# Maxima matmuls of an attention kernel with 32 rows instead of 64, and a Q image without zero rows

## The chip, the cores and the metric

The kernel runs on one NeuronCore of one Trainium2 chip. The metric is device time in microseconds (us), the median of repeated runs. Before the change it is 1701.23 us, the median of three runs (1700.1 to 1705.75).

## The reference, cut to what matters

The model is one "macaron" layer over 8 sequences of 512 tokens with 128 features: half a feed-forward block, an attention block, and the same feed-forward block again. The feed-forward block is itself an attention with 16 heads of 8 features over the whole sequence, followed by a mixture of 8 experts of which each token uses one.

```
def block(x):                       # _L0_ffn_ref
    x = x + _msa(_layernorm(x, ln1_w, ln1_b), w_qkv, w_proj)
    x = x + _moe_mlp(_layernorm(x, ln2_w, ln2_b), gate_w, gate_b, w1, w2)
    return x
x = x + 0.5 * block(_layernorm(x))
x = x + _L0_attn_ref(_layernorm(x), w_q, w_k, w_v, w_o)    # 16 heads, 4 of keys, RoPE
x = x + 0.5 * block(_layernorm(x))
```

Each attention is softmax(q k^T / sqrt(8)) v, for 16 heads with 8 features, on 512 queries and 512 keys, in float32. There are 3 x 8 = 24 such attentions in all, each of 16 heads.

## The kernel before, in words

The program is a setup, a `stream` of 8 sequences (first block), `experts`, a `stream` of 16 (the attention block and the second block's attention), `experts` again, and `finish`. The change touches only `stream` and the buffers it uses.

Inside `stream`, the 16 heads of a sequence are handled in G = 4 groups of J = 4 heads. One group of one sequence is a "head group" n; the first stream has 32 of them and the second 64. For each head group the kernel makes two passes over the scores:

- The maxima pass (`max_score`, L687): for each of 4 blocks of 128 queries (`qt`) and each of the 4 heads j, one matmul of Q against all 512 keys. VectorE then takes the row maxima of two such 128x512 results in one instruction (`take_max`, L1032).
- The score pass (`score`, L703): the transposed product, 128 keys against 512 queries, with the negative maxima already inside it. ScalarE exponentiates each result (L1008), and the matmuls of `weigh` (L715) multiply the probabilities with V.

Q and K of a head occupy rows of the 128-row memory. Heads with j even lie in rows 0 to 63, those with j odd in rows 64 to 127 (`TILE = 64`). Of each 64 rows, the first 32 (`ROWS = 4 * HD`) hold the 8 features of the head four times over, as high and low parts in every combination, which gives float32 precision from the faster `float32r` matmul. Rows 32 and 33 of Q hold the high and low part of the maxima, and all rows of K from 32 on hold -1, so the score matmul subtracts the maximum for free. The score pass must multiply these rows. The maxima pass, which runs before the maxima exist, must not see an old maximum there: `parts(j)` gives it all 64 rows, and the Q image that is loaded for each head group has 48 rows (`IMAGE`), of which the last 16 are zeros. To supply them, a DMA issued by ScalarE at the start (L979) writes zeros into the DRAM scratch `q_scratch`, SyncE waits for it (`zeroed`, L537), and SyncE writes zeros for the first head group by hand (L540), once per stream.

The order on each engine is written out. On TensorE, `step(n, kt)` is the steady state and has two half-steps. Each half-step issues two score matmuls of head group n and two maxima matmuls of head group n + 2, in the order maxima, score, maxima, score (or score, maxima, score, maxima), on alternating 64-row halves, and then the eight recorded passes of half a `weigh`. So there are 8 half-steps in a head group, 96 head groups, and 768 half-steps; in the last two head groups of each stream there is no later group, so 736 half-steps mix both kinds. `group(n, kt)` adds other work between the steps (transposes, projections, gate). Two maxima results go to VectorE per half-step, two score results to ScalarE. The maxima of head groups 0 and 1 are made ahead of the first step, without scores between them.

SyncE loads each head group's Q and K (`load`) four groups ahead, and writes the maxima into rows 32 and 33 of Q (`rows_of_max`, L524).

Of the kernel before, what the change touches and what calls it, by code (L numbers as in the profile page):

```python
# [19 lines left out]
F32 = mybir.dt.float32  # L20
# [6 lines left out]
P = 128  # L27
# [5 lines left out]
NG = B * G  # L33
# [9 lines left out]
KSLOT = PAIRS * S  # L43
TILE = 64
ROWS = 4 * HD
IMAGE = 48
VCOLS = G * QT * J * V1
VSLOTS = 3
RING = 4
# [3 lines left out]
SLOTS = 5  # L53
# [292 lines left out]
def stream(nc, c, a, label, kinds):  # L346
# [6 lines left out]
    with ExitStack() as ctx:  # L353
# [18 lines left out]
        def parts(j):  # L372

            r = TILE * (j % 2)
            return slice(r, r + TILE)

        def mcol(n, j, qt):

            return 16 * (n % 2) + 8 * (j % 2) + 4 * (j // 2) + qt
# [116 lines left out]
        @block.sync  # L496
        def _(sp):
            def load(n):
                if n >= SLOTS:
                    sp.wait_ge(s.scores, QT * J * (n - SLOTS + 1))  # L500
                g = n % SLOTS
                if n == 1 or n % G == 0:
                    stored(sp, 0, n // G + 1)
                for tile in range(2):
                    sp.dma_start(c.Q[TILE * tile:TILE * tile + IMAGE, g * KSLOT:(g + 1) * KSLOT].bitcast(F32),
                                 c.q_scratch[n % NG, tile, :, :]).then_inc(s.q_loaded[g], 16)
                if n == 1 or n % G == 0:
                    stored(sp, 1, n // G + 1)
                for tile in range(2):
                    for copy in range(2):  # L510
                        r = TILE * tile + 2 * HD * copy
                        sp.dma_start(c.K[r:r + 2 * HD, g * KSLOT:(g + 1) * KSLOT].bitcast(F32),
                                     c.k_scratch[n % NG, tile, :, :]).then_inc(s.k_loaded[g], 16)

            def rows_of_max(n):

                g = n % SLOTS
                if n:
                    released(sp, "rows", n)
                else:  # L520
                    sp.wait_ge(s.first, 2)
                for tile in range(2):
                    r = TILE * tile + ROWS
                    sp.dma_start(c.Q[r:r + 2, g * KSLOT:(g + 1) * KSLOT].bitcast(F32).rearrange("i (a n) -> i a n", n=P),  # L524
                                 c.maxT[16 * tile:16 * tile + 16, n % 2 * P:(n % 2 + 1) * P].bitcast(F32))\
                        .then_inc(s.max_rows[g], 16)

            if gathers:
                for b in range(EARLY + 1):
                    load_outputs(sp, c, b, s.gathered[b])  # L530
            later = later_loads(c, a) if label == 0 else []
            if label == 0:
                for b in range(1, B):
                    load_x(sp, c, a, b)
                sp.wait_ge(c.q_clear, 1)
                sp.wait_ge(c.k_clear, 1)
                sp.wait_ge(c.zeroed, 16)  # L537
            for tile in range(2):
                r = TILE * tile + ROWS
                sp.dma_start(c.Q[r:r + IMAGE - ROWS, 0:KSLOT].bitcast(F32).rearrange("r (o d) -> r o d", o=8),  # L540
                            c.zero[0:IMAGE - ROWS, :].rearrange("r (o d) -> r o d", o=1).broadcast_to((IMAGE - ROWS, 8, KSLOT // 8))).then_inc(s.q_loaded[0], 16)
            whole_ready(sp, 0, 0)
            straight(sp, 0, 0)
            for i in range(2):
                sp.wait_ge(s.lo[i], 1)
                straight(sp, i, 1)
            for i in range(2):
                store(sp, i, 0, s.first_stored[i], (1,))
            for n in range(1, 4):
                load(n)  # L550
            rows_of_max(0)
            for n in range(last):
                if n + 1 < last:
                    rows_of_max(n + 1)
                if n + 4 < last:
                    load(n + 4)
                if n == 0 and label == 0:
                    late_loads(sp, c, a)
                if n >= 1 and later:
                    dst, src = later.pop(0)  # L560
                    sp.dma_start(dst, src).then_inc(c.rest, 16)
            for g in range(SLOTS):
                sp.wait_ge(s.max_rows[g], 32 * len(range(g, last, SLOTS)))
            if label == 0:
                sp.wait_ge(c.rest, 16 * len(later_loads(c, a)))
            write_tails(sp, 0)
            sp.wait_ge(s.tails, 16 * E)
# [104 lines left out]
        def _(pe):  # L672
# [8 lines left out]
            def fill(ins, *name):  # L681
                t = turns[name]
                ins.then_inc(s.filled, t.end - t.first)

            def max_score(n, qt, j):
                bank = bank_for("max", n, qt, j)
                fill(nc.tensor.matmul(bank, q4[parts(j), n % SLOTS, j // 2, qt * P:(qt + 1) * P],  # L687
                                      k4[parts(j), n % SLOTS, j // 2, :], start=True, stop=True), "max", n, qt, j)

            def turn_max(n):  # L690

# [128 lines left out]
                        project(kind, i)  # L820

            def loaded(n):
                pe.wait_ge(s.q_loaded[n % SLOTS], 32 * (n // SLOTS + 1) + 128 * (n % SLOTS == 0))
                pe.wait_ge(s.k_loaded[n % SLOTS], 64 * (n // SLOTS + 1) + 64 * (n % SLOTS == 0))

            def maxima(n, qt):
# [47 lines left out]
        def _(act):  # L874
# [99 lines left out]
                act.wait_ge(c.weights, 16 * c.first_loads)  # L974
            if label:
                nc.scalar.activation(c.warm[:, :], c.zero[:, 0:1], ACT.Sqrt)
            else:
                act.wait_ge(c.x_loaded[0], 16)
                act.dma_start(c.q_scratch[:, :, ROWS:IMAGE, :].rearrange("g t r n -> (g t) (r n)"),  # L979
                              c.zero[:, :].rearrange("p (o d) -> p o d", o=1).broadcast_to((P, 16 * NG * (IMAGE - ROWS) // P, KSLOT // 8)))\  # L980
                    .then_inc(c.zeroed, 16)
            def roots(b):
                for i in range(1 + plan.ffn(b)):
                    act.wait_ge(s.var_ready, sum(1 + plan.ffn(x) for x in range(b)) + i + 1)
# [408 lines left out]
def build(nc, a, out):  # L1393
    with ExitStack() as ctx:
# [6 lines left out]
        c.x_loaded = [ctx.enter_context(nc.semaphore(f"x_loaded{b}")) for b in range(B)]  # L1401
        c.late_loads = 3
        c.q_clear, c.k_clear, c.v_clear = (ctx.enter_context(nc.semaphore(n)) for n in ("q_clear", "k_clear", "v_clear"))
        c.rest, c.zeroed = ctx.enter_context(nc.semaphore("rest")), ctx.enter_context(nc.semaphore("zeroed"))
        c.X, c.Y, c.N = sb("X", [P, B * S]), sb("Y", [P, B * S]), sb("N", [P, NT * W])
        c.rows = c.N[:, :].rearrange("p (t w) -> p t w", w=W)
        c.Q, c.K = (sb(n, [P, SLOTS * KSLOT], F32R) for n in ("Q", "K"))
# [9 lines left out]
        c.rstd, c.root, c.minus_half = sb("rstd", [P, 2 * QT]), sb("root", [P, 2 * QT]), sb("minus_half", [P, QT])  # L1417
        c.normed, c.zT, c.swap, c.turned, c.added = (sb(n, [P, S]) for n in ("normed", "zT", "swap", "turned", "added"))
        c.full, c.hi, c.lo = (sb(n, [P, 2 * S]) for n in ("full", "hi", "lo"))
        c.zero = sb("zero", [P, KSLOT // 8])  # L1420
        c.ident, c.upper, c.ones = sb("ident", [P, P]), sb("upper", [P, P]), sb("ones", [P, P])
        c.maxima = sb("maxima", [P, 32])
        c.split = sb("split", [P, 64], F32R)
# [10 lines left out]
        c.blocks, c.thresh, c.down = sb("blocks", [P, NBLK]), sb("thresh", [P, NT]), sb("down", [P, E])  # L1434
        c.banks = banks = ctx.enter_context(nc.psum_tensor("banks", [P, 8 * 512], F32))
        c.bank = [banks[:, i * 512:(i + 1) * 512] for i in range(8)]
        c.q_scratch = nc.dram_tensor("q_scratch", [NG, 2, IMAGE, KSLOT], F32).ap()
        c.k_scratch = nc.dram_tensor("k_scratch", [NG, 2, 2 * HD, KSLOT], F32).ap()
        c.sorted_x = nc.dram_tensor("sorted_x", [E * REGION + E * P, W], F32).ap()
        c.by_token = nc.dram_tensor("by_token", [NT * P + 2 * E * P, D], F32).ap()  # L1440
# [59 lines left out]
```

## Time and profile before

| | us |
|---|---|
| median of three runs | 1701.23 |
| the profiled execution, own time | 1694.1 |
| its span | 1692.4 |
| TensorE matmul busy | 1440.0 (85%) |
| TensorE weight loads busy | 657.9 (39%) |
| VectorE busy | 1212.0 (72%) |
| ScalarE busy | 1097.7 (65%) |
| GpSimd busy | 625.1 (37%) |

Durations come from one profiled execution, whose own time is 1.7 us more than its span and 7.1 us below the median.
### The profile page before, as it was taken

What the parts mean: (1) busy time and instruction counts of PE and PEld (TensorE: products, weight loads), DVE (VectorE), ACT (ScalarE), POOL (GpSimd) and SP (SyncE); (2) the same over time, 40 slices, a digit from 0 to 9 for tenths busy, and PEclk for the clock granted to TensorE, in tenths of its full rate; (3) what the DMA queues carried; (4) which work ended last, traced back from release to release, by engine and by line L of the source; (5) the groups of instructions that cost most, each with busy time, mean ns of one, the idle gap of its engine ahead of it and who ended that gap; (6) DMA issues with size and microseconds to landing.
All of it is one profiled execution on the core that took longest, in us unless ns stands there. A gap on an engine that the chain in (4) does not pass through costs nothing. (4 is left out here: it accounts for less than half of the span.)

```text
span 1692.4 us, 34258 instructions
## 1 busy us (share of the span) xinstructions
PE 1440.0 (85%) x11860; PEld 657.9 (39%) x11860; DVE 1212.0 (72%) x1961; ACT 1097.7 (65%) x2048; POOL 625.1 (37%) x964
## 2 busy tenths in 40 slices
PE   1899999998964992699999999999999999992994
PEld 1333333333333771233333333333343343332673
DVE  4788888888812444588888888888888888853334
ACT  1377877777742431288888888887877777770441
POOL 2323254432242341454444452233334452125332
PEclk8599999999976995699999999999999999995997
DMA  6545443442001212433324334334234333201114
GB/s 189 121 109 123 105 99 84 108 112 66 24 8 48 57 49 71 107 94 79 94 76 104 91 86 102 87 75 99 64 86 96 92 76 79 55 9 33 53 55 120
DMA packets 99543, 139.07 MB, mean 82 GB/s; under 512 B 26160, under 2 KB 69936, under 8 KB 99376
## 3 DMA queue, kind: packets, MB, share of 16 engines
q1 hardware_dynamic: 60768, 82.65, 19.4%
q0 software_dynamic: 24016, 45.57, 10.8%
q10 hardware_dynamic: 14592, 8.67, 1.7%
q8 instruction: 100, 1.64, 0.4%
q14 instruction: 67, 0.55, 0.1%
HBM read 78.64 MB, written 55.23 MB: 79 GB/s over the span
## 5 line engine op out<-in xcount | busy, mean ns | idle before, releaser
L1032 DVE TENSOR_REDUCE maxima<-banks 128x2 f32<-128x1024 f32 x768 | 923.9, 1222 | 190.4 <-PE banks L687 184.9
L1008 ACT ACTIVATE work<-banks 128x512 f32<-128x512 f32 x1536 | 828.7, 597 | 132.7 <-PE banks L703 119.3
L687 PE MATMUL banks<-K,Q 64*128 64x512 f32 x1536 | 574.6, 463 | 70.9 <-DVE maxima L1032 33.8
L703 PE MATMUL banks<-Q,K 64*128 64x512 f32 x1536 | 571.3, 453 | 11.3 <-ACT work L1008 10.6
L715 PE MATMUL banks<-work,V 128*9 128x256 f32 x6144 | 478.0, 383 | 1.9 <-ACT work L1008 0.8
L687 PEld LDWEIGHTS banks<-K,Q 64*128 64x128 f32 x1536 | 230.7, 190 | 229.5 <-DVE maxima L1032 109.9
L703 PEld LDWEIGHTS banks<-Q,K 64*128 64x128 f32 x1536 | 230.1, 186 | 196.3 <-issue 134.3
L715 PEld LDWEIGHTS banks<-work,V 128*9 128x9 f32 x6144 | 91.4, 88 | 276.5 <-issue 210.7
L1350 DVE COPY work<-banks 128x512 f32<-128x512 f32 x80 | 55.3, 692 | 130.0 <-PE banks L1298 125.7
L612 POOL TENSOR_TENSOR lo<-full,hi 128x512 fp32r<-128x512 f32 x44 | 56.3, 1280 | 246.5 <-issue 97.6
L1272 POOL DMA_INDIRECT by_token<-work x80 | 76.6, 957 | 151.2 <-DVE work L1355 150.5
L105 POOL TENSOR_SCALAR root<-moments 128x4 f32<-128x4 f32 x36 | 8.4, 232 | 272.2 <-DVE moments L1108 190.4
L1328 ACT ACTIVATE work<-banks,ln 128x128 f32<-128x128 f32 x80 | 36.6, 457 | 96.8 <-PE banks L1286 96.8
L1292 PE MATMUL banks<-w,work 128*128 x160 | 92.4, 660 | 1.2 <-ACT work L1328 0.5
L1306 PE MATMUL banks<-w,work 128*128 x640 | 84.8, 275 | 0.3 <-issue 0.3
L1334 ACT ACTIVATE work<-banks 128x512 f32<-128x512 f32 x80 | 47.8, 597 | 47.6 <-PE banks L1292 38.9
L1306 PEld LDWEIGHTS banks<-w,work 128*128 128x128 f32 x640 | 77.7, 192 | 0.7 <-issue 0.7
L599 POOL DMA_INDIRECT sorted_x<-N,pos x64 | 64.3, 1004 | 28.1 <-issue 14.6
L619 POOL TENSOR_TENSOR Y<-Y,added 128x512 f32<-128x512 f32 x16 | 20.6, 1286 | 129.3 <-ACT added L933 129.3
L724 PE MATMUL banks<-ident,outT 128*128 128x128 f32 x384 | 62.8, 286 | 6.2 <-DVE maxima L1032 4.6
L901 ACT ACTIVATE full<-banks 128x512 f32<-128x512 f32 x48 | 28.7, 597 | 58.8 <-PE banks L742 58.0
L883 ACT ACTIVATE outT<-banks 128x512 f32<-128x512 f32 x96 | 58.2, 606 | 2.3 <-PE banks L715 2.3
(172 smaller groups left out, 1354.5 us busy)
## 6 DMA issues: line engine op xcount, KB each, us to landing
Q<-q_scratch SPq DMA_DIRECT2D x188, 192.0 KB, 3.5
K<-k_scratch SPq DMA_DIRECT2D x376, 64.0 KB
q_scratch<-hi POOLq DMA_DIRECT2D x44, 256.0 KB, 4.7
q_scratch<-lo POOLq DMA_DIRECT2D x44, 256.0 KB, 6.8
k_scratch<-hi POOLq DMA_DIRECT2D x22, 256.0 KB, 4.6
k_scratch<-lo POOLq DMA_DIRECT2D x22, 256.0 KB, 6.4
work<-sorted_x SPq DMA_DIRECT2D x80, 66.0 KB
q_scratch<-zero ACTq DMA_DIRECT2D x1, 4096.0 KB, 19.7
```

The lines of the kernel that those rows point to most:

```text
L599: nc.gpsimd.indirect_dma_start(c.sorted_x[:, :], bass.IndirectOffsetOnAxis(ap=c.pos[:, t:t + 1], axis=0), c.rows[:, t, :], None).then_inc( ...
L612: nc.gpsimd.tensor_tensor(lo[i].bitcast(F32R), full[i], hi[i], ALU.subtract).then_inc(s.lo[i], 1)
L687: fill(nc.tensor.matmul(bank, q4[parts(j), n % SLOTS, j // 2, qt * P:(qt + 1) * P], k4[parts(j), n % SLOTS, j // 2, :], start=True, stop=T ...
L703: nc.tensor.matmul(scp[x % EXPS][:, :], k4[parts(j), n % SLOTS, j // 2, kt * P:(kt + 1) * P], q4[parts(j), n % SLOTS, j // 2, :], start=Tr ...
L715: ins = nc.tensor.matmul(outp[32 * j:32 * j + V1, q], v4[:, n // G % VSLOTS, kt, n % G, j, :], prob[:, kt, j, q], start=(kt == 0 and half ...
L724: ins = nc.tensor.transpose(bank[:, t * P:(t + 1) * P], c.outT[:, t * P:(t + 1) * P], c.ident[:, :])
L883: nc.scalar.activation(c.outT[:, :], outp[:, :], ACT.Copy).then_inc(s.out_copied, 1)
L1008: nc.scalar.activation(prob[:, kt, j ^ 1, :], scp[x % EXPS][:, :], ACT.Exp, scale=SCALE).then_inc(s.probs, 1)
L1032: nc.vector.tensor_reduce(c.maxima[:, at:at + 9:8], c.banks[:, k * S:(k + 2) * S].rearrange("p (m n) -> p m n", m=2), AX.X, ALU.max).then_ ...
L1272: nc.gpsimd.indirect_dma_start(c.by_token[:, :], bass.IndirectOffsetOnAxis(ap=x_sb[i % ring][:, D:D + 1].bitcast(U32), axis=0), y_sb[i % r ...
L1292: nc.tensor.matmul(hp[i % 2][:, :], uT[i % 2], cols(c.w1, at, HID), start=True, stop=True).then_inc(s.hidden, 1)
L1306: ins = nc.tensor.matmul(yp[i % 2][:, 0:D], hT[i % 2][:, t * P:(t + 1) * P], cols(c.w2, at + t * D, D), start=(t == 0), stop=(t == HT - 1))
```

## The change

The maxima matmuls use a new slice `heads(j)`, the first 32 rows of each half, where old maxima can't reach them. The Q image in DRAM and each load of it shrink from 48 to 32 rows (192 KB to 128 KB). The ScalarE DMA that writes zeros, the SyncE wait for it, and the four SyncE DMAs of zeros are gone; the count that TensorE waits for in slot 0 is adapted. The score matmuls still use 64 rows.

```
+        def heads(j):
+            r = TILE * (j % 2)
+            return slice(r, r + ROWS)
...
-                    sp.dma_start(c.Q[TILE * tile:TILE * tile + IMAGE, g * KSLOT:(g + 1) * KSLOT].bitcast(F32),
+                    sp.dma_start(c.Q[TILE * tile:TILE * tile + ROWS, g * KSLOT:(g + 1) * KSLOT].bitcast(F32),
                                  c.q_scratch[n % NG, tile, :, :]).then_inc(s.q_loaded[g], 16)
...
                 sp.wait_ge(c.k_clear, 1)
-                sp.wait_ge(c.zeroed, 16)
-            for tile in range(2):
-                r = TILE * tile + ROWS
-                sp.dma_start(c.Q[r:r + IMAGE - ROWS, 0:KSLOT]...,
-                            c.zero[0:IMAGE - ROWS, :]...).then_inc(s.q_loaded[0], 16)
             whole_ready(sp, 0, 0)
             straight(sp, 0, 0)
...
-                fill(nc.tensor.matmul(bank, q4[parts(j), n % SLOTS, j // 2, qt * P:(qt + 1) * P],
-                                      k4[parts(j), n % SLOTS, j // 2, :], start=True, stop=True), "max", n, qt, j)
+                fill(nc.tensor.matmul(bank, q4[heads(j), n % SLOTS, j // 2, qt * P:(qt + 1) * P],
+                                      k4[heads(j), n % SLOTS, j // 2, :], start=True, stop=True), "max", n, qt, j)
...
-                pe.wait_ge(s.q_loaded[n % SLOTS], 32 * (n // SLOTS + 1) + 128 * (n % SLOTS == 0))
+                pe.wait_ge(s.q_loaded[n % SLOTS], 32 * (n // SLOTS + (n % SLOTS > 0)) + 128 * (n % SLOTS == 0))
...
-            else:
-                act.wait_ge(c.x_loaded[0], 16)
-                act.dma_start(c.q_scratch[:, :, ROWS:IMAGE, :]..., c.zero[:, :]...).then_inc(c.zeroed, 16)
...
-        c.q_scratch = nc.dram_tensor("q_scratch", [NG, 2, IMAGE, KSLOT], F32).ap()
+        c.q_scratch = nc.dram_tensor("q_scratch", [NG, 2, ROWS, KSLOT], F32).ap()
```

The order of TensorE's instructions stays as it was. This is the changed kernel's TensorE program at an early step of the first stream; `L686` is `max_score` (L687 before), `L702` is `score` (L703 before), `L714` is `weigh` (L715 before), and 128x512 is the size of the result:

```order
L686 MATMUL banks<-K,Q 128x512
L702 MATMUL banks<-Q,K 128x512
L686 MATMUL banks<-K,Q 128x512
L702 MATMUL banks<-Q,K 128x512
L714 MATMUL banks<-work,V 9x256 x4
L702 MATMUL banks<-Q,K 128x512
L686 MATMUL banks<-K,Q 128x512
L702 MATMUL banks<-Q,K 128x512
L686 MATMUL banks<-K,Q 128x512
L714 MATMUL banks<-work,V 9x256 x4
```

Nothing moved here: 32-row and 64-row matmuls now alternate where all four were 64-row ones.

On SyncE, at the start of the first stream, this stood before (`Q<-zero` are the zeros, `Q<-hi`, `Q<-lo` and `K<-lo` the first head group, the loads from `q_scratch` and `k_scratch` the second):

```order
L137 DMA X<-in_x 128x4x128 x7
L540 DMA Q<-zero 16x8x128 x2
L410 DMA Q<-hi 8x2x512 x4
L410 DMA Q<-lo 8x2x512 x4
L410 DMA K<-lo 8x2x512 x4
L401 DMA q_scratch<-lo 8x16x512 x2
L401 DMA k_scratch<-lo 8x16x512
L505 DMA Q<-q_scratch 48x1024 x2
```

and this stands there now:

```order
L136 DMA X<-in_x 128x4x128 x7
L414 DMA Q<-hi 8x2x512 x4
L414 DMA Q<-lo 8x2x512 x4
L414 DMA K<-lo 8x2x512 x4
L405 DMA q_scratch<-lo 8x16x512 x2
L405 DMA k_scratch<-lo 8x16x512
L509 DMA Q<-q_scratch 32x1024 x2
```

The two DMAs of zeros are gone, and everything behind them has moved up; the wait that stood ahead of them is gone too.

## Rows read from the trace of the kernel before

**Rows 1.** The page, costliest groups: busy, mean ns, idle before.
```profile
L1032 DVE TENSOR_REDUCE maxima<-banks 128x2 f32<-128x1024 f32 x768 | 923.9, 1222 | 190.4 <-PE banks L687 184.9
...
L687 PE MATMUL banks<-K,Q 64*128 64x512 f32 x1536 | 574.6, 463 | 70.9 <-DVE maxima L1032 33.8
...
L715 PE MATMUL banks<-work,V 128*9 128x256 f32 x6144 | 478.0, 383 | 1.9 <-ACT work L1008 0.8
```
**Rows 2.** Timeline, 1044 to 1050 us, TensorE's weight loads: start, length, line.
```profile
1044.53 0.97 PEld L749 LDWEIGHTS banks<-wv_ffn,zT 128*128 128x128 f32 x8
1045.62 0.18 PEld L687 LDWEIGHTS banks<-K,Q 64*128 64x128 f32 x1
...
1045.74 0.19 PEld L687 LDWEIGHTS banks<-K,Q 64*128 64x128 f32 x1
1046.29 0.12 PEld L715 LDWEIGHTS banks<-work,V 128*9 128x9 f32 x8 [0.36 <-issue]
1046.84 0.18 PEld L703 LDWEIGHTS banks<-Q,K 64*128 64x128 f32 x1 [0.43 <-issue]
...
1048.05 0.18 PEld L687 LDWEIGHTS banks<-K,Q 64*128 64x128 f32 x1 [0.43 <-issue]
```
**Rows 3.** The same stretch, TensorE's matmuls.
```profile
1044.15 0.66 PE L724 MATMUL banks<-ident,outT 128*128 128x128 f32 x4
1044.64 1.06 PE L749 MATMUL banks<-wv_ffn,zT 128*128 128x128 f32 x8
1045.63 0.50 PE L687 MATMUL banks<-K,Q 64*128 64x512 f32 x1
...
1045.96 0.39 PE L687 MATMUL banks<-K,Q 64*128 64x512 f32 x1
1046.29 0.62 PE L715 MATMUL banks<-work,V 128*9 128x256 f32 x8
```
**Rows 4.** Timeline near 320.6 us: a matmul, then the weight load after it.
```profile
320.60 0.27 PE L694 MATMUL banks<-ident,split 128*32 128x128 f32 x1 [0.88 <-DVE maxima L1032]
...
320.69 0.30 PEld L793 LDWEIGHTS banks<-onehot,upper 128*128 128x128 f32 x2
```
**Rows 5.** Timeline of VectorE, the first maxima of all.
```profile
42.75 9.14 DVE L1032 TENSOR_REDUCE maxima<-banks 128x2 f32<-128x1024 f32 x8 [9.83 <-PE banks L687]
```
**Rows 6.** Windows: PE, PEld, DVE, ACT, POOL busy, clock, DMA; then L1032 alone.
```profile
727.00:1499.00 772.00, 729.57 (x6590) 293.53 (x6590) 663.55 (x969) 621.21 (x1157) 310.85 (x474) 1.00 0.34 85
...
727.00:1499.00 772.00, 581.38 (x483) 1.00 0.34 85
```
**Rows 7.** Timeline of SyncE's queue at the start of the first stream.
```profile
25.47 1.80 SPq L540 DMA_DIRECT2D Q<-zero  x2
27.31 7.07 SPq L410 DMA_DIRECT2D Q<-hi  x4
34.43 2.81 SPq L410 DMA_DIRECT2D Q<-lo  x4
```
**Rows 8.** The same stretch: ScalarE, VectorE and TensorE.
```profile
18.53 0.59 ACT L903 ACTIVATE hi<-banks 128x512 fp32r<-128x512 f32 x1
...
32.53 0.38 DVE L1108 BATCH_NORM_AGGREGATE moments<-stats 128x2 f32<-128x6 f32 x4
...
41.84 1.22 PE L687 MATMUL banks<-K,Q 64*128 64x512 f32 x4 [20.42 <-issue]
```
**Rows 9.** SyncE's queue, the second stream's first data.
```profile
658.83 2.97 SPq L410 DMA_DIRECT2D Q<-hi  x4
```
**Rows 10.** Windows and timeline around a fall of TensorE's clock.
```profile
264.00:267.80 3.80, 2.56 (x23) 1.45 (x23) 3.07 (x9) 2.11 (x6) 2.54 (x7) 1.00 0.00 0
267.80:271.20 3.40, 3.40 (x24) 0.87 (x22) 1.52 (x2) 2.44 (x5) 2.99 (x6) 0.50 0.40 99
...
268.58 1.04 PE L715 MATMUL banks<-work,V 128*9 128x256 f32 x8
269.55 0.79 PE L703 MATMUL banks<-Q,K 64*128 64x512 f32 x1
```

More of the change, by code:

```diff
@@ L45 @@
 ROWS = 4 * HD
-IMAGE = 48
 VCOLS = G * QT * J * V1
@@ L536, in _ @@
                 sp.wait_ge(c.k_clear, 1)
-                sp.wait_ge(c.zeroed, 16)
-            for tile in range(2):
-                r = TILE * tile + ROWS
-                sp.dma_start(c.Q[r:r + IMAGE - ROWS, 0:KSLOT].bitcast(F32).rearrange("r (o d) -> r o d", o=8),
-                            c.zero[0:IMAGE - ROWS, :].rearrange("r (o d) -> r o d", o=1).broadcast_to((IMAGE - ROWS, 8, KSLOT // 8))).then_inc(s.q_loaded[0], 16)
             whole_ready(sp, 0, 0)
@@ L976, in _ @@
                 nc.scalar.activation(c.warm[:, :], c.zero[:, 0:1], ACT.Sqrt)
-            else:
-                act.wait_ge(c.x_loaded[0], 16)
-                act.dma_start(c.q_scratch[:, :, ROWS:IMAGE, :].rearrange("g t r n -> (g t) (r n)"),
-                              c.zero[:, :].rearrange("p (o d) -> p o d", o=1).broadcast_to((P, 16 * NG * (IMAGE - ROWS) // P, KSLOT // 8)))\
-                    .then_inc(c.zeroed, 16)
             def roots(b):
@@ L1403, in build @@
         c.q_clear, c.k_clear, c.v_clear = (ctx.enter_context(nc.semaphore(n)) for n in ("q_clear", "k_clear", "v_clear"))
-        c.rest, c.zeroed = ctx.enter_context(nc.semaphore("rest")), ctx.enter_context(nc.semaphore("zeroed"))
+        c.rest = ctx.enter_context(nc.semaphore("rest"))
         c.X, c.Y, c.N = sb("X", [P, B * S]), sb("Y", [P, B * S]), sb("N", [P, NT * W])
@@ L1419, in build @@
         c.full, c.hi, c.lo = (sb(n, [P, 2 * S]) for n in ("full", "hi", "lo"))
-        c.zero = sb("zero", [P, KSLOT // 8])
+        c.zero = sb("zero", [P, 1])
         c.ident, c.upper, c.ones = sb("ident", [P, P]), sb("upper", [P, P]), sb("ones", [P, P])
```

## The prediction

> **What bounds the kernel now.** I read the page first, then TensorE's timeline in one steady stretch, then VectorE's, then the windows, and last the start of each stream.
>
> By busy time the page makes VectorE's row maxima (923.9 us) look like the bound, and the matmuls of the maxima pass and of `weigh` (574.6, 478.0) like feeders. The idle columns say otherwise: VectorE waited 190.4 us ahead of its maxima, 184.9 of it for the maxima matmuls, while those waited only 33.8 us for VectorE [rows 1]. So TensorE is at least as late as VectorE.
>
> The timeline shows why. A half-step starts with the weight load at 1046.84 and the next one at 1048.05 [rows 2]: 1.21 us. It has two parts. From 1045.62 to 1046.29, 0.67 us, two pairs of 512-column matmuls run, a score and a maxima matmul beside each other on rows 0 to 63 and 64 to 127; the second pair loads its weights at 1045.74, long before the first pair ends at 1045.63 + 0.50 [rows 2, 3]. From 1046.29 to 1046.84, 0.55 us, `weigh` runs. VectorE could go a little faster than 1.21: at the start, where TensorE has nothing but maxima to make, eight reductions of 1.22 take 9.14 us, (9.14 - 1.22) / 7 = 1.13 us from one to the next [rows 1, 5]. The two engines are nearly tied, with TensorE the later by 0.08 us. Where a group's extra work stands in the order, TensorE waits for VectorE instead: in the stretch 727 to 1499 it is idle for 772.0 - 729.6 = 42.4 us, over 483 / 8 = 60 head groups [rows 6], 0.7 us each, 67 us over all 96. So a gain for TensorE of more than 0.08 us per half-step would be useless, but a loss is paid nearly in full, 736 times.
>
> **The change, part by part.**
>
> *The maxima matmuls with 32 rows.* The numbers of columns, 128 to load and 512 to stream, stay. In the trace a `weigh` matmul of 128 rows and 256 columns isn't longer than a 64-row one of 512 (383 and 463 ns) [rows 1]; nothing says that fewer rows are faster, and I expect no shorter instruction. What changes is the company. In the rows a weight load follows a matmul whose weights have another number of rows three times, and each time it holds back until 0.06 to 0.08 us before that matmul's recorded end: 128x128 to 64x128 (load at 1045.62, end 1044.64 + 1.06 = 1045.70), 64x128 to 128x9 (1046.29 against 1045.96 + 0.39 = 1046.35), and 128x9 to 64x128 (1046.84 against 1046.29 + 0.62 = 1046.91) [rows 2, 3]. Where the number of rows stays, it doesn't hold back: L749's loads begin at 1044.53 while L724's matmuls run until 1044.81, the second pair's load at 1045.74 falls into the first pair, on the very rows in use, and even a change of columns alone, 128x32 to 128x128, loads at 320.69 into a matmul that ends at 320.87 [rows 2 to 4]. So it is the change in the number of rows that empties the array, not rows in use. After the edit each of the four matmuls differs in it from the one before (32, 64, 32, 64, then 128). I take it that they then run one by one.
>
> The price of a lone matmul: its record from the load's start to the end is 0.50 us and the next load starts some 0.07 to 0.08 before that [rows 2, 3], so 0.42 us. A half-step becomes 4 x 0.42 + 0.55 = 2.23 us instead of 1.21, 1.02 more, and 736 mixed half-steps 751 us more. Bounds: nothing at all below (two row counts at once never occur in this trace), and above the case that load and matmul each stand alone, 0.18 + 0.39 = 0.57 [rows 2, 3], 2.83 per half-step, 1192 us in all. I take 0.42, since all three changes in the rows go by it. The 32 half-steps without maxima, and the maxima made ahead of each stream, keep one row count and don't change.
>
> The Trainium skill, page "TensorEngine Tiling (Array Packing)", section "Key Properties", says that changing the tiling mode, not just the tile, drains TensorE. The rows agree for the rows' mode and not for the columns' one; by that rule the sum is the one above. The same skill's page "TensorE: Matmul & The Clock Gate", section "The mechanism", speaks for a free edit: a weight load overlaps matmuls in flight only when its row group differs, and the partners of a pair differ in it. By it the time would be that of rival B. The trace contradicts this rule in one respect, since the second pair loads onto rows in use without a wait; no row shows two row counts on separate rows.
>
> *What the longer half-step hides.* At 2.23 us VectorE (1.22) has slack, and the 67 us in which TensorE waits, mostly for VectorE's backlog, mostly go. Between 0 and 67, I take 50 off, since a part of the waits is latency and remains.
>
> *The start of the first stream.* SyncE issues the first rows of Q at 27.31, right behind the two DMAs of zeros at 25.47, which waited for the scratch write [rows 7]. The high part of Q is complete at 18.53 + 0.59 = 19.12 [rows 8]. So this step moves up by 8.2 us, and its four DMAs may need 2.81 us like the next four instead of 7.07: TensorE's first maxima could come up to 12.5 us before 41.84. But VectorE, which must take them, has its own work until 32.53 + 0.38 = 32.91 and began its maxima at 42.75 [rows 5, 8], so at most 9.8 us come through. I take 9; the least is 0, if the 256 KB stores that follow prove the late ones.
>
> *The start of the second stream.* The two DMAs of zeros stand ahead of a wait for data that ends at 658.83 [rows 9]: nothing.
>
> *The smaller Q loads.* 188 loads carry 64 KB less each. They are issued four head groups ahead, 4 x 772 / 60 = 51 us [rows 6], and longer half-steps only give them more cover: nothing.
>
> *The sum*, against the profiled execution: 1694 + 751 - 50 - 9 = 2386 us. The median of the runs lies 7 us above that execution, so 2393; I say 2390.
>
> **The rivals.**
>
> *A. Row counts hold each other back only where they share rows.* Then the maxima matmul on rows 0 to 31 runs beside the score matmul on rows 64 to 127, but the second pair, whose rows and shapes are swapped, waits for the first: 2 x 0.42 + 0.55 = 1.39 us, 0.18 more, 132 us in all. VectorE keeps pace with less slack, so perhaps 25 us of waits go: 1694 + 132 - 25 - 9 + 7 = 1799 us. For it: all changes of the row count in the trace share rows. Against it: sharing alone costs nothing there.
>
> *B. A change from 64 to 32 rows costs nothing*, and the start decides: 1694 - 9 + 7 = 1692 us, faster. The place is the first 42 us, the price up to 9.8 us. It holds if the price of a mixed half-step is under 9 / 736 = 0.01 us. For it: loads are pulled ahead freely within one shape, and 32 rows would then only leave more of the array free. Against it: three changes of the row count, three waits.
>
> *C. The clock falls as well.* In the stretch 264.0 to 267.8 TensorE is busy for 2.56 of 3.80 us, with long gaps, and after it the granted clock is 0.50 for 3.4 us [rows 10]. The new half-steps are dense in records but have half as many columns per microsecond. At the lower level a lone matmul takes 0.79 - 0.07 = 0.72 us and `weigh` 269.55 - 268.58 = 0.97 [rows 10], a half-step 4 x 0.72 + 0.97 = 3.85. All the time at that level would make 2.64 x 736 = 1943 us on top of 1694 - 50 - 9 + 7, 3585 us; half of the time, about 2990. Against it: the new half-steps leave no gap between records, and the stretch that made it fall had waits of about a microsecond.
>
> **How the numbers follow.** The forecast, one by one at the full clock, 0.62; A 0.12; B 0.13; C 0.13. The forecast's own range is 2340 (all 67 us of waits gone, 0.41 per matmul) to 2830 (0.57). Adding A on the low side and the mild part of C on the high side gives 1780 to 2900, which leaves out B and the strong part of C. A measurement of this kernel tells 0.3%, some 5 us, from no change. Faster is B less a start that brings little: 0.12. Same is the rest of it and a little of A: 0.03. Slower 0.85.
>
> **What would show it.** In the changed kernel's timeline, the four matmuls of a half-step should start 0.42 us apart, none beside another; a half-step should take 2.23 us; VectorE should wait about 1 us before each of its maxima, always for the maxima matmul, and its wait ahead of them should rise from 190 us to some 800; the mean granted clock should stay near 0.93 or above. The first maxima should start near 30 us. If pairs still start together, A or B holds, and the distance between the first and the second pair tells which: 0.42 for A, 0.11 for B. A half-step of over 3 us with the clock at 0.50 is C. I am wrong altogether if the median is under 2000.

## The result, and the profile after

The changed kernel takes 3581.6 us, the median of four runs (3562.5 to 3601.8), against 1703.5 us for the kernel before, run beside it: a ratio of 2.103, 95% interval 2.092 to 2.115. The forecast was 2390 us with a range of 1780 to 2900. The direction was right, the size was not. The profiled execution took 3564.6 us with a span of 3562.9. Single executions are now and then far slower than the others of the same kernel (one of the kernel before took 1965.4 us, one of e6 below 4254.6), and all ratios leave those out.

The page shows the same five kinds of work. The columns are those of [rows 1]; the last line is TensorE's granted clock in 40 equal slices, in tenths.

```profile
L1026 DVE TENSOR_REDUCE maxima<-banks 128x2 f32<-128x1024 f32 x768 | 939.7, 1226 | 1932.9 <-PE banks L686 1932.9
...
L686 PE MATMUL banks<-K,Q 32*128 32x512 f32 x1536 | 1142.4, 759 | 37.2 <-DMA K<-lo 27.0
L702 PE MATMUL banks<-Q,K 64*128 64x512 f32 x1536 | 1132.4, 748 | 3.1 <-ACT work L1002 3.1
L714 PE MATMUL banks<-work,V 128*9 128x256 f32 x6144 | 765.8, 589 | 1.1 <-ACT work L1002 0.8
...
PEclk6555555555557955555555555555555555555578
```

VectorE's wait for the maxima matmuls rose from 184.9 us [rows 1] to 1932.9. The busy time of the maxima matmuls doubled, from 574.6 to 1142.4 us, for two reasons. Their records no longer overlap one another: before, 1536 x 463 ns = 711 us of records lay within 574.6 us [rows 1], now 1536 x 759 ns = 1166 us lie within 1142.4. And the larger part: one matmul went from 463 to 759 ns, which being alone does not explain, since at the full clock a lone one takes 0.50 us (below). The clock line stands at 5 through both streams. The mean granted clock of the run is 0.564, against 0.930 before. The digits 7 and 9 in the middle of the line and 7 and 8 at its end are the `experts` stages, which take as long as before: from the last `weigh` of the first stream to the first of the second it is 227.1 us (225.7 before).

One stretch of TensorE's timeline shows both effects, since the clock rises and falls inside it (start, length, line):

```profile
1355.89 0.79 PE L686 MATMUL banks<-K,Q 32*128 32x512 f32 x1
1356.61 0.50 PE L702 MATMUL banks<-Q,K 64*128 64x512 f32 x1
1357.04 0.50 PE L686 MATMUL banks<-K,Q 32*128 32x512 f32 x1
1357.47 0.49 PE L702 MATMUL banks<-Q,K 64*128 64x512 f32 x1
1357.89 0.62 PE L714 MATMUL banks<-work,V 128*9 128x256 f32 x8
...
1360.18 1.04 PE L714 MATMUL banks<-work,V 128*9 128x256 f32 x8
1361.15 0.79 PE L686 MATMUL banks<-K,Q 32*128 32x512 f32 x1
1361.87 0.79 PE L702 MATMUL banks<-Q,K 64*128 64x512 f32 x1
1362.59 0.79 PE L686 MATMUL banks<-K,Q 32*128 32x512 f32 x1
1363.31 0.79 PE L702 MATMUL banks<-Q,K 64*128 64x512 f32 x1
1364.03 1.04 PE L714 MATMUL banks<-work,V 128*9 128x256 f32 x8
1365.00 0.79 PE L702 MATMUL banks<-Q,K 64*128 64x512 f32 x1
```

The four matmuls of a half-step start one after the other: 0.43 us apart where the clock is 1.00 (1357.04 to 1357.47), 0.72 apart where it is 0.50 (1361.15 to 1361.87). From 1357.89 to 1360.18, at the full clock, a half-step takes 2.29 us. From 1361.15 to 1365.00, at half the clock, it takes 3.85 us. The full clock lasts for less than two half-steps here, from about 1356.6 to 1360.1, and it falls with no gap in TensorE's records before it.

The windows say how much of the run is like the second kind (columns as in [rows 6]; the second line is the maxima reductions alone):

```profile
1300.00:2000.00 700.00, 699.70 (x2228) 251.48 (x2228) 231.75 (x306) 238.42 (x402) 121.11 (x137) 0.52 0.11 31
...
1300.00:2000.00 700.00, 202.26 (x165) 0.52 0.11 31
```

TensorE is idle for 0.3 us of 700, and yet the clock averages 0.52. There is one reduction per half-step, so one half-step with its share of all other work takes 700 / 165 = 4.24 us, against 772.0 / 483 = 1.60 before [rows 6]. Over the whole of the second stream (1305.7 to 3394.6) TensorE is idle for 0.1% and the clock averages 0.53.

The start of the first stream did move up (SyncE's queue, then TensorE):

```profile
20.76 3.03 SPq L414 DMA_DIRECT2D Q<-hi  x4
...
26.66 5.70 SPq L414 DMA_DIRECT2D K<-lo  x4
...
35.44 1.22 PE L686 MATMUL banks<-K,Q 32*128 32x512 f32 x4 [12.85 <-DMA K<-lo]
```

TensorE's first maxima start at 35.44 instead of 41.84 [rows 8], 6.4 us earlier. What they wait for last is the landing of `K<-lo`.

### The profile page after: what moved, and what is told of

It reads as the page before. It is cut to its first block and busy times, and to the rows that moved or that the text cites. A ratio compares the mean times of both kernels' runs of the same rounds, so it can differ in the third digit from the quotient of the medians.

```text
span 3562.9 us, 34253 instructions
## 1 busy us (share of the span) xinstructions
PE 3384.8 (95%) x11860; PEld 1336.9 (38%) x11860; DVE 1254.1 (35%) x1961; ACT 1198.4 (34%) x2048; POOL 623.3 (17%) x964
## 5 line engine op out<-in xcount | busy, mean ns | idle before, releaser
L1026 DVE TENSOR_REDUCE maxima<-banks 128x2 f32<-128x1024 f32 x768 | 939.7, 1226 | 1932.9 <-PE banks L686 1932.9
L1002 ACT ACTIVATE work<-banks 128x512 f32<-128x512 f32 x1536 | 912.0, 597 | 1609.6 <-PE banks L702 1604.6
L686 PE MATMUL banks<-K,Q 32*128 32x512 f32 x1536 | 1142.4, 759 | 37.2 <-DMA K<-lo 27.0
L702 PE MATMUL banks<-Q,K 64*128 64x512 f32 x1536 | 1132.4, 748 | 3.1 <-ACT work L1002 3.1
L714 PE MATMUL banks<-work,V 128*9 128x256 f32 x6144 | 765.8, 589 | 1.1 <-ACT work L1002 0.8
L686 PEld LDWEIGHTS banks<-K,Q 32*128 32x128 f32 x1536 | 408.7, 272 | 772.7 <-issue 706.7
L702 PEld LDWEIGHTS banks<-Q,K 64*128 64x128 f32 x1536 | 408.3, 269 | 765.6 <-ACT work L1002 420.0
L714 PEld LDWEIGHTS banks<-work,V 128*9 128x9 f32 x6144 | 96.9, 94 | 319.8 <-issue 303.2
L723 PE MATMUL banks<-ident,outT 128*128 128x128 f32 x384 | 104.2, 425 | 1.6 <-ACT outT L882 1.6
L723 PEld LDWEIGHTS banks<-ident,outT 128*128 128x128 f32 x384 | 66.9, 212 | 80.4 <-issue 80.4
L464 POOL TENSOR_TENSOR before<-before,onehot 128x8 f32<-128x8 f32 x48 | 9.6, 201 | 349.2 <-DVE onehot L1141 346.4
```

The lines of the kernel that those rows point to most:

```text
L686: fill(nc.tensor.matmul(bank, q4[heads(j), n % SLOTS, j // 2, qt * P:(qt + 1) * P], k4[heads(j), n % SLOTS, j // 2, :], start=True, stop=T ...
L702: nc.tensor.matmul(scp[x % EXPS][:, :], k4[parts(j), n % SLOTS, j // 2, kt * P:(kt + 1) * P], q4[parts(j), n % SLOTS, j // 2, :], start=Tr ...
L714: ins = nc.tensor.matmul(outp[32 * j:32 * j + V1, q], v4[:, n // G % VSLOTS, kt, n % G, j, :], prob[:, kt, j, q], start=(kt == 0 and half ...
L723: ins = nc.tensor.transpose(bank[:, t * P:(t + 1) * P], c.outT[:, t * P:(t + 1) * P], c.ident[:, :])
L1002: nc.scalar.activation(prob[:, kt, j ^ 1, :], scp[x % EXPS][:, :], ACT.Exp, scale=SCALE).then_inc(s.probs, 1)
L1026: nc.vector.tensor_reduce(c.maxima[:, at:at + 9:8], c.banks[:, k * S:(k + 2) * S].rearrange("p (m n) -> p m n", m=2), AX.X, ALU.max).then_ ...
```

## The experiments

Fourteen kernels were run, in four groups: e1 to e4, e5 to e8, e9 to e12, e13 and e14. Each group has its own runs of the kernel before beside it (median 1685 us in the first group, 1704 in the second, 1683 in the third, 1704 in the fourth), so ratios compare better than times. The expectations reckon with 1701. "T" below is the theory after the result: a change of row count makes matmuls run alone, and at that spacing the clock does not hold.

### The 32 rows alone (e1)

```
 # the kernel before, and only this:
-q4[parts(j), ...], k4[parts(j), ...]      # in max_score
+q4[heads(j), ...], k4[heads(j), ...]
```

> The kernel before, with the maxima matmuls on 32 rows and nothing else of the change. Theory (the row count alternates, each matmul then runs alone, and at that density the clock stays at 1.2 GHz): all of the loss is here, 3580 to 3600 us, mean clock 0.56, a mixed half-step of 3.85 us. Rival (a part of the loss comes from the Q image, the missing zeros or the changed counts): well under 3500.

Measured: 3591.3 us, ratio 2.134 (2.129 to 2.139), clock 0.561. The whole loss is this one slice. The rival is out.

### The image alone (e2)

```
 # the changed kernel, with
-q4[heads(j), ...], k4[heads(j), ...]
+q4[parts(j), ...], k4[parts(j), ...]
```

> The changed kernel with the maxima matmuls on 64 rows again, so old maxima enter them (that reset is left out, and the exponentials use a small scale to stay finite; no duration depends on it). Theory: half-steps of 1.21 us, clock 0.93, and the start of the first stream 6 to 7 us earlier: 1694 to 1698 us. Rival (the image part has a cost of its own, or the start is hidden): 1703 or more.

Measured: 1676.8 us, ratio 0.9945 (0.9931 to 0.9960), clock 0.931. The image part gains some 9 us (8.4 by the two medians, 9.4 by the ratio on 1701), close to the forecast's step for the start and a little more than was expected here, where 1694 on 1701 is a ratio of 0.996. TensorE's first maxima stand at 33.94 in its timeline, 7.9 us earlier than before, and the 17th reduction of VectorE still starts 7.9 us earlier (62.5 against 70.4):

```profile
33.94 1.22 PE L686 MATMUL banks<-K,Q 64*128 64x512 f32 x4 [13.41 <-DMA K<-lo]
```

### 32 rows beside 32, then 64 beside 64 (e3)

```
 # the changed kernel, in step
 for half in range(2):
-    (maxima, score, maxima, score)
+    if m < last:
+        for i in range(2): max_score(m, kt, 2 * half + i)     # 32 rows
+    for j in (2 * half + 1, 2 * half): score(n, kt, j)        # 64 rows
```

> The changed kernel with the order of a half-step changed to maxima, maxima, score, score: partners of a pair have one row count, and one change of it is left inside the half-step instead of three. Theory: the pairs run beside each other again, 0.42 + 0.42 + 0.55 = 1.39 us per half-step at 2.4 GHz, and with the array filled the clock holds: 1790 to 1810 us, clock over 0.9. Rival (32-row matmuls as such make the clock fall, whatever their neighbours): the clock near 0.56 again, half-step 0.72 + 0.72 + 0.97 = 2.41 us, about 2550 us.

Measured: 1768.0 us, ratio 1.046 (1.042 to 1.050), clock 0.922. TensorE's timeline, where x2 means that two start together:

```profile
1045.06 0.50 PE L686 MATMUL banks<-K,Q 32*128 32x512 f32 x2
1045.48 0.50 PE L702 MATMUL banks<-Q,K 64*128 64x512 f32 x2
1045.91 0.62 PE L714 MATMUL banks<-work,V 128*9 128x256 f32 x8
1046.46 0.50 PE L686 MATMUL banks<-K,Q 32*128 32x512 f32 x2
```

The half-step is 1.40 us (1045.06 to 1046.46), with 0.42 and 0.43 for the pairs. The same instructions in another order halve the time of the program: the loss is neither the 32-row matmul nor its duration, it is the company. The clock rival is out in its strong form. By the ratio, too, the program is faster than expected (1790 on 1701 would be 1.052); e11 says why.

### A smaller image with zeros (e4)

```
-IMAGE = 48
+IMAGE = 34
```

> The kernel before with a Q image of 34 rows instead of 48: only the two rows that old maxima occupy are reset, the others stay zero from the first clear. The write of zeros is 8 times smaller. Theory: row counts stay 64, nothing else changes, the start gains 6 to 8 us: 1694 to 1698 us. Rival (the odd row count makes the loads slower, or the start is bound elsewhere): 1700 or more.

Measured: 1681.8 us, ratio 0.9987 (0.9977 to 0.9998). A gain of 2 to 3 us, less than expected, though TensorE's first maxima stand at 33.74, as early as in e2. The trace shows where the rest stays. At the start of each stream TensorE has made the maxima of the first head group and then waits for the loads of Q for the second:

```profile
48.03 1.22 PE L687 MATMUL banks<-K,Q 64*128 64x512 f32 x4 [3.37 <-issue]
673.34 1.22 PE L687 MATMUL banks<-K,Q 64*128 64x512 f32 x4 [4.17 <-DMA Q<-q_scratch]
```

The view of these loads puts both waits, 7.5 us, down to them; e2, with loads of 32 rows, has no such wait (its matmuls follow at 44.79, without a gap). At the 17th reduction e4 is 3.2 us behind e2, and its span is 3.4 us longer. Why loads of 34 rows arrive later is open.

### Isolated mixed half-steps (e5, e6)

```
 # the kernel before, in max_score; e6 leaves out "and j < 2"
+rows = heads(j) if qt == 0 and j < 2 else parts(j)
-q4[parts(j), ...], k4[parts(j), ...]
+q4[rows, ...], k4[rows, ...]
```

> The kernel before, with 32 rows for the two maxima matmuls of one half-step in eight (first query block, heads 0 and 1): 92 isolated mixed half-steps between dense ones. Theory (each change of row count costs a drain, and the clock falls only where thin half-steps follow one another): the clock holds, a mixed half-step takes the 2.23 us that were forecast, 1.02 more, 94 us in all less some 15 of hidden waits: 1755 to 1775 us, clock over 0.9. Rival (a single mixed half-step already makes the clock fall): some 1900.

Measured: 1756.0 us, ratio 1.032 (1.027 to 1.036), clock 0.932. Here is the half-step as forecast, undisturbed:

```profile
1041.56 0.50 PE L693 MATMUL banks<-K,Q 32*128 32x512 f32 x1
1041.99 0.50 PE L709 MATMUL banks<-Q,K 64*128 64x512 f32 x1
1042.42 0.49 PE L693 MATMUL banks<-K,Q 32*128 32x512 f32 x1
1042.85 0.49 PE L709 MATMUL banks<-Q,K 64*128 64x512 f32 x1
1043.27 0.62 PE L721 MATMUL banks<-work,V 128*9 128x256 f32 x8
1043.82 0.50 PE L709 MATMUL banks<-Q,K 64*128 64x512 f32 x1
```

It takes 2.26 us (1041.56 to 1043.82), against 2.23 forecast. 92 of them at 2.26 - 1.21 would cost 97 us; the program lost 52, three times as much hidden as the 15 us expected, and the time is at the low edge (1.032 x 1701 = 1755). Of the other 45 us the traces show 25 as waits of TensorE that are gone: over both streams it is idle for 70 us before and for 45 here. Where the other 20 are hidden the traces don't say.

> The same for two half-steps in eight, one after the other (first query block, all four heads): 184 mixed half-steps. Theory: 188 us less some 30 of hidden waits if the clock holds through 4.5 us of thin work, 1835 to 1850 us; where it falls, each pair of mixed half-steps and its neighbours run at 1.2 GHz for one interval of the trace, 3.2 us more, 2100. This run is to tell which. Rival (32-row matmuls as such): the same 2100.

Measured: 1899.5 us, ratio 1.113 (1.107 to 1.119), clock 0.892. Two mixed half-steps in a row cost 196 us instead of 2 x 52. The gross price, 184 x 1.05 = 193 us, is cut by the waits that it hides, in e5 some 45 us, so about that much is left for the clock, whose mean fell from 0.932 in e5 to 0.892. The result lies between the two cases of the expectation, and the trace says why: the clock falls 37 times in the two streams, for 3.4 or 6.8 us each, so after some of the 92 pairs and not after all. In e5 it falls once in the streams, after TensorE had been idle for 1.5 of 3.8 us.

### 128-row maxima against 64-row scores (e7, e13)

```
 # the changed kernel, in max_score; e13 also resets the rows of old maxima, as e12
-q4[heads(j), ...], k4[heads(j), ...]
+q4[0:P, ...], k4[0:P, ...]
```

> The changed kernel with the maxima matmuls on all 128 rows (both heads of the tile at once; the maxima are not the reference's, and the exponentials use a tiny scale to stay finite). Scores keep 64 rows, so 128 and 64 alternate. Theory (any change of the row count makes matmuls run alone, and what matters for the clock is how much of the time columns stream): the same as 32 and 64, half-step 3.85 us, clock 0.56, 3560 to 3600 us. Rival (the clock falls because 32-row matmuls occupy little of the array): the clock holds with 128 rows, half-step 2.23 us, 2370 us. A second rival (32 rows are special, 128 and 64 can share): 1690 us.

Measured: two executions, 2461.4 us at a clock of 0.910 and 2514.5 at 0.886, against 1703.8. The trace is of the slower one. The spacing is that of e5, with nothing overlapping:

```profile
1500.89 0.50 PE L686 MATMUL banks<-K,Q 128*128 128x512 f32 x1
1501.32 0.50 PE L702 MATMUL banks<-Q,K 64*128 64x512 f32 x1
1501.75 0.51 PE L686 MATMUL banks<-K,Q 128*128 128x512 f32 x1
```

T fails here in its second half. The row count alternates and matmuls run alone, 0.43 apart, so the first half stands; but the clock mostly holds, as the first rival said. Since old maxima entered these products and grew from slot to slot, the data could have been the cause, so it was repeated without them:

> The run with 128-row maxima once more, without its odd data: the two rows with old maxima are reset before each load, so the products stay of ordinary size (the maxima are still those of two heads together, exponentials with a small scale). Theory (rows in use kept the clock up): clock 0.85 to 0.93 and 2370 to 2500 us, as with the grown data. Rival (the growing values in rows 32 and 96 did it, and rows in use don't matter): near 0.56 and 3580 us, or the 0.77 of the run with 128-row scores.

Measured: 2461.8 us, ratio 1.445 (1.440 to 1.450), clock 0.913, the same as e7's faster execution. The grown values are out as a cause. Another rival stays untested: e7, e8, e9 and e13 shrink the exponent, so the probabilities that `weigh` reads are all close to 1, which is not so in the changed kernel and e1. (e2 shrinks it too and has the clock of the kernel before, 0.931, but its matmuls are dense.)

### All matmuls on 128 rows (e8)

```
 # e7, and the same in score
-k4[parts(j), ...], q4[parts(j), ...]
+k4[0:P, ...], q4[0:P, ...]
```

> Maxima and score matmuls both on all 128 rows (neither is the reference's, exponentials with a tiny scale). Nothing can run beside another, but the row count never changes, in `weigh` neither. Theory: loads are pulled ahead, the four matmuls start 0.21 to 0.22 us apart instead of 0.42, half-step 1.4 to 1.6 us, clock holds: 1850 to 1980 us. Rival (what costs the 0.42 is that nothing runs beside it, not the change of row count): 2.23 us per half-step or more, over 2350 us.

Measured: 1940.8 us, ratio 1.140 (1.134 to 1.146), clock 0.947.

```profile
1103.87 0.50 PE L702 MATMUL banks<-Q,K 128*128 128x512 f32 x1
1104.21 0.39 PE L686 MATMUL banks<-K,Q 128*128 128x512 f32 x1
1104.44 0.40 PE L702 MATMUL banks<-Q,K 128*128 128x512 f32 x1
1104.67 0.40 PE L686 MATMUL banks<-K,Q 128*128 128x512 f32 x1
1105.00 0.62 PE L714 MATMUL banks<-work,V 128*9 128x256 f32 x8
1105.55 0.50 PE L686 MATMUL banks<-K,Q 128*128 128x512 f32 x1
```

Nothing can run beside anything here, yet matmuls start 0.23 us apart (1104.21, 1104.44, 1104.67) instead of 0.43: with one shape, being alone costs 0.23, and the change of row count the other 0.20. The half-step is 1.68 us (1103.87 to 1105.55), a little over the 1.4 to 1.6 expected, because `weigh` still waits although its row count is 128 too: it starts at 1105.00, 0.07 before the end at 1104.67 + 0.40. The first matmul behind `weigh` waits likewise (1105.55 against 1105.00 + 0.62). So "only the row count matters", which the prediction drew from [rows 4], is too narrow; from 128x128 to the four 9-column blocks of `weigh` the array is emptied as well. The trace of the kernel before had it already, in the other direction (a matmul, then the next weight load):

```profile
474.44 0.62 PE L715 MATMUL banks<-work,V 128*9 128x256 f32 x8
...
474.99 0.30 PEld L793 LDWEIGHTS banks<-onehot,upper 128*128 128x128 f32 x2 [0.43 <-issue]
```

Both have 128 rows, and the load still comes only 0.07 us before the end at 475.06.

### The other side: scores on 128 rows, maxima on 32 (e9)

```
 # the changed kernel, in score
-k4[parts(j), ...], q4[parts(j), ...]
+k4[0:P, ...], q4[0:P, ...]
```

> The changed kernel with the scores on all 128 rows and the maxima on 32 (scores not the reference's, exponentials with a tiny scale). Same spacing as 32 and 64, since the row count alternates. What the 128-row maxima run left standing: with the same number of matmuls and columns, rows in use decide whether the clock holds. Theory (rows in use count): between the 0.56 of 32 and 64 rows and the 0.89 of 128 and 64, so 2500 to 3200 us, with the half-step 2.25 us wherever the clock is 1.00. Rival (only the maxima's 32 rows are to blame, whatever the scores do): 0.56 and 3580 us. Rival (data, not rows, kept the clock up in the other run): 0.56 as well.

Measured: 2826.2 us, ratio 1.679 (1.671 to 1.686), clock 0.768. Same spacing, same count and size of results, and the clock stands between the two others. In one order, for the whole run: 32 and 64 rows 0.564 (0.561 in e1), 32 and 128 rows 0.768, 64 and 128 rows 0.910 and 0.913 (e7's faster execution, e13). e7 and e9 have the same exponent, so between these two the close-to-1 probabilities are no difference. TensorE's idle share goes the other way: in the second stream it is 0.1% at a clock of 0.53 (the changed kernel), 0.7% at 0.79 (e9) and 1.1% at 0.95 (e13).

### All matmuls on 32 rows (e10)

```
 # the changed kernel, in score
-k4[parts(j), ...], q4[parts(j), ...]
+k4[heads(j), ...], q4[heads(j), ...]
```

> The changed kernel with the scores on 32 rows too (the maxima aren't subtracted; exponentials with a small scale). The row count never changes inside the pairs, and fewer rows are in use than in any other run, but densely. Theory (the loss needs lone matmuls, a change of row count makes them): pairs run beside each other, half-step 1.21 us, 1675 to 1700 us, clock over 0.9. Rival (32-row matmuls make the clock fall by themselves): half-step 1.9 us or more, over 2100 us.

Measured: two executions, 1742.4 us at a clock of 0.890 and 1776.9 at 0.865, against 1683.3. The faster one, of which the trace is, has a ratio of 1.035. Partners overlap, as T says. But the ratio is 4 to 5% over the expected (0.985 to 0.999), and there are long stretches at half the clock:

```profile
1302.98 0.79 PE L686 MATMUL banks<-K,Q 32*128 32x512 f32 x1
1302.99 0.79 PE L702 MATMUL banks<-Q,K 32*128 32x512 f32 x1
...
1305.11 0.79 PE L702 MATMUL banks<-Q,K 32*128 32x512 f32 x1
```

These half-steps take 2.13 us (1302.98 to 1305.11). The windows show how the stretch begins and ends (columns as in [rows 6]):

```profile
1296.00:1299.80 3.80, 2.56 (x23) 1.45 (x21) 2.74 (x7) 2.14 (x5) 2.90 (x7) 1.00 0.00 0
1299.80:1310.00 10.20, 10.20 (x60) 4.55 (x58) 5.46 (x6) 4.40 (x9) 4.73 (x11) 0.50 0.17 55
1310.00:1314.00 4.00, 4.00 (x41) 1.52 (x40) 3.08 (x5) 3.66 (x7) 1.28 (x1) 1.00 0.00 0
```

The clock falls behind the same gap in TensorE's work as in [rows 10], 2.56 us busy of 3.80. With 64 rows it was back after 3.4 us, both times that it fell within a stream of the kernel before; here, in dense work, it stays down for 10.2. Over both streams that makes 170 us at half the clock, against 12 before. So with fewer rows alone the clock was less steady: it came back later after a gap. In the changed kernel it fell without any gap.

### The order alone (e11), and two versions for use (e12, e14)

e11 is the kernel before with e3's order. e12 keeps 64-row maxima and the 32-row image, and resets the two rows of old maxima with small DMAs. e14 is both.

```
 # e12, in load(n) on SyncE, after each Q load (and once for slot 0)
+sp.dma_start(c.Q[r:r + 2, slot]..., c.zero[0:2, :] repeated 8 times).then_inc(s.q_loaded[g], 16)
```

> The control for the regrouped run: the kernel before, 64 rows throughout, with only the order maxima, maxima, score, score. Theory: pairs of whatever kind run beside each other as long as all have 64 rows, so the order is worth nothing: ratio 0.995 to 1.005. Then the 4.6% that the regrouped 32-row kernel lost are all row changes. Rival (the order itself costs, since VectorE gets its pair at another moment): over 1.01.

Measured: 1660.3 us, ratio 0.986 (0.985 to 0.988). This expectation was wrong: the order is worth 23 us. VectorE's wait for the maxima matmuls fell from 184.9 [rows 1] to 129.5 us:

```profile
L1030 DVE TENSOR_REDUCE maxima<-banks 128x2 f32<-128x1024 f32 x768 | 924.0, 1222 | 135.1 <-PE banks L687 129.5
```

With both maxima in the first pair of a half-step, VectorE's pair is complete one pair, some 0.34 us, earlier. That this is how the 23 us come about is read from the order and the wait, not tested by itself. It also explains e3: 1.046 / 0.986 = 1.060 is what the 32 rows and the image make together without the order, inside the 1.052 to 1.064 that T had expected; with the image's 0.9945 taken out as well, the row changes cost a factor of 1.066.

> A version that should beat both: the 32-row Q image and no write of zeros at the start, 64-row maxima, and the two rows with old maxima reset by two small DMAs per load, from a tile of zeros. Theory: the earlier start (6 to 8 us) and nothing else, ratio 0.993 to 0.997. Rival (376 more DMA issues on SyncE delay the loads or the maxima rows): 1.00 or more.

Measured: 1675.5 us, ratio 0.9950 (0.9935 to 0.9966): as expected, and the gain of e2 with the right maxima.

> The two gains together: 32-row Q image with the reset by small DMAs, 64-row maxima, and the order maxima, maxima, score, score. Theory: they lie in different places (the start, and VectorE's waits in the steady state) and add up: 0.9950 x 0.9864 = 0.9815, so 0.979 to 0.984. Rival (the earlier start is eaten where the denser stream now waits for loads): 0.986.

Measured: 1670.3 us against 1703.5, ratio 0.981 (0.978 to 0.984). The two gains add up. This is the fastest version, 1.9% under the kernel before.

## Why the prediction was wrong, point by point

**The step that failed** is the choice of the clock: "The forecast, one by one at the full clock, 0.62; ... C 0.13". At the full clock a half-step was to take 2.23 us; nearly all of the run's take 3.85, at a mean clock of 0.53 to 0.54 in the two streams. Rival C, with the clock at its lower level throughout, said 3585 us, and 3582 was measured. Its term was 2.64 us for each of 736 half-steps, and the windows show 4.24 - 1.60 = 2.64 for a half-step with its share of other work. That they agree to the last digit is luck, since the bare half-step (3.85 - 1.21) leaves out that other work slows down too, and that the clock is high for some of the time. The argument against C was that "the new half-steps leave no gap between records". That was true and did not matter: TensorE was recorded idle for 0.3 us of 700 and stood at 0.52. I had read the fall of the clock in [rows 10] as an effect of idle gaps, which it may be (e10's falls come behind such gaps too), and took unbroken records for a clock that holds. What in the new half-steps brings the clock down is shown in part: with lone matmuls at one spacing it went with the rows in use (e9 against e7 and e13); the data that `weigh` reads are not ruled out as a part of it.

**The row count and the lone matmuls: right.** Four matmuls in a row, 0.42 forecast and 0.42 to 0.43 measured (e5), half-step 2.23 forecast and 2.26 measured. Where the clock nearly held under this spacing (e13), the program took 758 us more, where the forecast's sum had 751 - 50 - 9 = 692. Rival A and rival B are out: partners on separate rows ran one after the other in e5, which no row before had shown. The Trainium skill, page "TensorEngine Tiling (Array Packing)", section "Key Properties", says that changing the tiling mode drains TensorE. e5's 0.43 us from start to start agrees. The Trainium skill, page "TensorE: Matmul & The Clock Gate", section "The mechanism", says that a load is pulled ahead of matmuls in flight when its row group does not conflict, or when it goes to the background weight buffer. The first half is contradicted here: rows 0 to 31 and 64 to 127 differ, and e5's loads did not overlap. The second half leaves room for the pairs' loads onto rows in use, which the prediction counted against the page.

**That it is only the row count: wrong.** The prediction says that where the number of rows stays, the load doesn't hold back. e8 shows `weigh` waiting at an equal row count, and so does the load at 474.99 in the trace before. The number of columns counts as well where `weigh` with its 9-column blocks is on one side; the one change of columns in [rows 4] was not enough to say that it never does. It had no effect on the sum, since each of the new changes is one of rows.

**No shorter instruction for 32 rows: right**, 0.50 us in e5 for 32 and 64 rows alike.

**Hidden waits: right.** 50 of 67 us forecast. In e13, where all half-steps are mixed and the clock nearly holds, TensorE is idle for 23 us over both streams against 70 before, so 47 went.

**The start: the size right, the path not.** 9 us forecast; e2 measured 8.4 to 9.4, e12 8. The first rows of Q moved up as forecast, by 8.0 us in e2 (to 19.28). But the first maxima started at 33.94 there and at 35.44 in the changed kernel, not near 30, and not VectorE's own work held them: they waited for `K<-lo`, whose four DMAs took 5.5 and 5.7 us to issue instead of 2.81 before. In the changed kernel that is 6.4 us earlier; there TensorE's first work of all also began 1.5 us later (15.39 against 13.85). The smaller loads and the second stream's start were put at nothing, and e2's 7.9 us at the start leave about a microsecond over for them.

**VectorE after the change.** It "should wait about 1 us" with a total of some 800 at the full clock; in e13, the nearest run at nearly the full clock, the total is 925, in the changed kernel 1933.

## What to carry to other kernels

Matmuls that are to overlap on separate rows need weights of one row count; when part of them can do with fewer rows, either group them by row count or leave the rows in and fill them with something harmless, since a column costs the same at 32 and at 64 rows (both pairs of e3 take 0.42 to 0.43 us). When a change thins out TensorE's work, price it at both levels of the clock, and do not argue from idle time alone: the changed kernel was idle for 0.1% of its second stream at 0.53, e13 for 1.1% at 0.95. Where two engines are nearly tied, it pays to try which result of a group comes first.

## What the runs showed of the hardware that was not expected

- At one spacing and with the same number of columns, the mean clock of the run followed the rows in use: 0.56 with 32 and 64 rows, 0.77 with 32 and 128, 0.91 with 64 and 128. TensorE was idle for about 1% of the second stream or less in all of them, and least where the clock was lowest. (The last two ran with probabilities close to 1, the first with real ones.)
- Behind the same gap (2.56 us busy of 3.80) the clock was down for 3.4 us with dense pairs of 64-row matmuls and for 10.2 us with dense pairs of 32-row ones (e10); the mean was 0.93 and 0.89.
- Two thin half-steps in a row (e6) lowered the clock 37 times at 92 such places; a single one (e5) left it up.
- With Q loads of 34 rows TensorE waited 7.5 us for them at the starts of the two streams (e4), with 32 rows (e2) not at all.
- With one shape of weights, matmuls on the same rows start 0.23 us apart; a change of the row count makes it 0.43, at the lower clock 0.72 (e8, e5, the changed kernel).
